# Cross-attention in 64 software-pipelined slots: u's halves made sooner, the mask on ScalarE, and the inputs of the first slots normalised ahead of A's turns

## The reference

```
# block 0: c = channels (128), t and s = positions (512)
Mn = Wn @ inorm(x) + bn;  Mm = Wm @ inorm(ctx) + bm
A  = softmax(Mn^T Mm)                        # 512 x 512, per item
x1 = Wo @ ((Wl @ ctx + bl) A^T) + bo + x
# block 1: 128 queries and 128 keys of 512 features, 16 heads of 32
q = layer_norm(x1) @ q_w + q_b;  k = ctx @ k_w + k_b;  v = ctx @ v_w + v_b
hidden = softmax(q k^T / sqrt(32), masked) v @ cproj_w + cproj_b + x1
out = hidden + gelu(layer_norm(hidden) @ fc_w + fc_b) @ proj_w + proj_b      # fc: 512 -> 2048
```

## Time and profile before

| | |
|---|---|
| median of 3 runs | 3034.93 us (3034.04 to 3037.51) |
| profiled execution | 3036.39 us, span 3034.5 us |
| granted clock of PE, mean | 0.984 of full speed |
| busy, share of the span | PE 94%, PE weight loads 78%, DVE 63%, ACT 48%, POOL 37% |
| DMA | 416.65 MB, mean 137 GB/s |

### The profile page before, as it was taken

One profiled execution on the slowest core, in us unless ns is written; L12 is line 12 of the kernel. 1 busy time (PEld: TensorE's weight loads), 2 busy tenths in 40 slices (PEclk: granted clock), 3 DMA queues, 4 the chain that ended last, 5 costly groups with the idle time before them and its releaser, 6 DMA issues. The chain is left out here.

```text
span 3034.5 us, 54536 instructions
## 1 busy us (share of the span) xinstructions
PE 2864.3 (94%) x17527; PEld 2369.3 (78%) x17527; DVE 1910.4 (63%) x3705; ACT 1469.5 (48%) x4210; POOL 1119.3 (37%) x998
## 2 busy tenths in 40 slices
PE   5899999999999999999977999999999999999999
PEld 3777777777777777777765888888888888888887
DVE  5799899999989899999855433333333333333332
ACT  5788778887878877888743211111111111111111
POOL 5566666666666666666632000000000000000000
PEclk7999999999999999999997999999999999999999
DMA  6588888888888888888863210101111111011110
GB/s 184 164 237 230 231 238 229 239 229 235 232 227 237 228 235 236 232 235 232 226 175 129 69 40 17 41 28 41 41 41 41 29 27 39 30 41 41 41 28 14
DMA packets 440889, 416.65 MB, mean 137 GB/s; under 512 B 155200, under 2 KB 319552, under 8 KB 440768
## 3 DMA queue, kind: packets, MB, share of 16 engines
q1 hardware_dynamic: 440768, 415.40, 49.4%
HBM read 231.79 MB, written 167.77 MB: 132 GB/s over the span
## 5 line engine op out<-in xcount | busy, mean ns | idle before, releaser
L1306 ACT ACTIVATE gl<-pre,fc_bias 128x512 f32<-128x512 f32 x256 | 176.6, 690 | 1119.4 <-PE pre L1391 1119.4
L1345 DVE CAST hT_hi<-gl 128x512 fp32r<-128x512 f32 x256 | 109.3, 427 | 840.2 <-ACT gl L1306 840.2
L673 ACT ACTIVATE rows<-bank,negmax 128x128 f32<-128x128 f32 x1024 | 364.2, 394 | 209.2 <-DVE negmax L829 198.9
L599 POOL TENSOR_TENSOR at_lo<-a_blocks,at_hi 128x512 fp32r<-128x512 f32 x256 | 335.4, 1330 | 190.1 <-ACT at_hi L710 190.1
L590 POOL TENSOR_TENSOR rows<-rows,rsum 128x512 f32<-128x512 f32 x256 | 266.0, 1040 | 271.4 <-DVE rsum L825 271.4
L177 POOL TENSOR_TENSOR rstd<-ve,neghalf 128x4 f32<-128x4 f32 x16 | 16.3, 1018 | 870.9 <-DVE ve L171 870.9
L1390 PE MATMUL pre<-yT_hi,rest_lo 128*128 128x512 f32 x768 | 298.9, 389 | 0.0
L1389 PE MATMUL acc<-rest_lo,hT_hi 128*128 128x512 f32 x768 | 298.9, 389 | 0.0
L1391 PE MATMUL acc<-rest_hi,hT_hi 128*128 128x512 f32 x768 | 298.9, 389 | 0.0
L1391 PE MATMUL pre<-yT_hi,rest_hi 128*128 128x512 f32 x768 | 298.8, 389 | 0.0
L1389 PE MATMUL pre<-yT_lo,rest_hi 128*128 128x512 f32 x768 | 298.8, 389 | 0.0
(11 more groups left out here) (158 smaller groups left out, 7886.1 us busy)
## 6 DMA issues: line engine op xcount, KB each, us to landing
a_turn<-rows SPq DMA_DIRECT2D x128, 512.0 KB, 7.6
a_blocks<-a_turn SPq DMA_DIRECT2D x256, 256.0 KB, 5.0
p_turn<-rows SPq DMA_DIRECT2D x128, 512.0 KB, 4.5
p_blocks<-p_turn SPq DMA_DIRECT2D x256, 256.0 KB, 5.9
x_ctx<-in_x SPq DMA_DIRECT2D x64, 256.0 KB, 2.6
x_ctx<-in_ctx SPq DMA_DIRECT2D x64, 256.0 KB, 2.9
blocks<-in_ctx SPq DMA_DIRECT2D x256, 64.0 KB, 5.5
small<-in_x SPq DMA_DIRECT2D x64, 256.0 KB, 5.9
```

The source lines that it names most:

```text
L599: pool.tensor_tensor(by_rows(at_lo, j), a_chunks[:, j], by_rows(at_hi, j).bitcast(F32), ALU.subtract).then_inc(at_lo_set, 1)
L673: act.activation(probs[:, :, r, c, :], by_chunk(S1_BANK[r])[:, c, :].rearrange("p (d b) -> p d b", b=32), ACT.Exp, bias=negmax1[:, r, c:c ...
L1306: act.activation(gl[:, i % 2, :], pre[i % 2][:], ACT.Gelu_apprx_tanh, bias=mlp.fc_bias[:, i:i + 1]).then_inc(gelu_done, 1)
```

## The change

Six edits:

1. ACT makes u_hi after the first of the four scalings of A, no longer after the fourth.
2. DVE makes u_lo ahead of the normalising of the next inputs and of the last two turns of A, no longer behind both.
3. The mask minus 1 moves from DVE to ACT, where it stands behind the upper halves of the next inputs and ahead of ctxT_hi. It takes a bias of -1 from a new constant, and the count of constants goes from 3 to 4.
4. In slots 0 to 4 (`filling`) DVE takes the statistics of the next inputs ahead of the maxima of S0, and normalises them right behind the inverted sums, ahead of A's turns.
5. In the same slots ACT makes their upper halves ahead of the scalings of A, and POOL their lower halves ahead of at_lo.
6. The halves of k's weights stand on POOL behind the lower halves of the inputs; those of v's weights, which stood at the head of slot 1 on ACT and POOL, stand on ACT behind M's halves and on POOL behind the lower halves of the inputs.

```diff
@@ POOL @@
+                filling = b0.exists() and not b4.exists()
...
-                if b0.first():
-                    lower_halves(K_W)
+                def lower_normed():
+                    if ahead.exists():
+                        for i in range(2):
+                            pool.wait_ge(normed_hi_set, ahead.nth(2, i + 1))
+                            pool.tensor_tensor(normed_lo[:, i, :], normed[:, i, :],
+                                               normed_hi[:, i, :].bitcast(F32), ALU.subtract).then_inc(normed_lo_set, 1)
...
+                if filling:
+                    lower_normed()
+                if b0.first():
+                    lower_halves(K_W)
+                if a1.first():
+                    lower_halves(V_W)
                 lower_at(0)
                 lower_at(1)
...
+                if not filling:
+                    lower_normed()
@@ ACT @@
                 if b0.first():
                     upper_halves(K_W)
+                if a1.first():
+                    upper_halves(V_W)
...
+                if filling:
+                    upper_normed()
                 if b0.exists():
                     act.wait_ge(rsum0_set, b0.nth(1, 1))
-                    for t in range(DC):
-                        act.activation(A[:, :, t, :], A[:, :, t, :], ACT.Identity,
-                                       scale=rsum0[:, t:t + 1]).then_inc(a_scaled, 1)
+                scale_a(0)
                 if b1.exists():
                     act.wait_ge(u_done, b1.nth(1, 1))
                     act.activation(u_hi, bank[U_BANK][:], ACT.Copy).then_inc(u_hi_set, 1)
+                scale_a(1)
+                scale_a(2)
+                scale_a(3)
                 upper_at(0)
...
+                if not filling:
+                    upper_normed()
+                if b3.exists():
+                    if b3.first():
+                        act.wait_ge(consts_set, 4)
+                    act.wait_ge(mask_loaded[b3.parity], b3.dma())
+                    if b3.has_before(1):
+                        act.wait_ge(s1_done, (b3 + -1).nth(1, 1))
+                    act.activation(mask_less_1[:], mask_u8[:, b3.parity, :], ACT.Identity,
+                                   bias=minus_one[:]).then_inc(mask_set, 1)
@@ DVE @@
+                if filling:
+                    input_statistics()
                 sum1_reciprocal(1)
...
-                if ahead.exists():
...
+                if not filling:
+                    input_statistics()
                 if b0.exists():
                     dve.wait_ge(exp0_done, b0.nth(4, 4))
                     if a1.exists():
                         dve.wait_ge(a_scaled, a1.nth(4, 4))
                     dve.reciprocal(rsum0[:], sum0[:]).then_inc(rsum0_set, 1)
+                if filling:
+                    normalise_inputs()
                 turn_a(0)
                 turn_a(1)
...
-                turn_a(2)
-                turn_a(3)
                 if b1.exists():
                     dve.wait_ge(u_hi_set, b1.nth(1, 1))
                     lower(u_lo, bank[U_BANK][:], u_hi, u_lo_set)
+                if not filling:
+                    normalise_inputs()
+                turn_a(2)
+                turn_a(3)
...
-                    dve.tensor_scalar(mask_less_1[:], mask_u8[:, b3.parity, :], -1.0, None,
-                                      ALU.add).then_inc(mask_set, 1)
```

More of the change, by code:

```diff
@@ L640, in first_group @@
                     mlp.lower_half(pool, mlp.first_lo[:, 1, c, :], mlp.first_hi[:, 1, c, :], 1, c, mlp_raw[1])
-            slots(pool, slot, {1: lambda: lower_halves(V_W), LAST: first_group})
+            slots(pool, slot, {LAST: first_group})
         @block.scalar
@@ L706, in slot, with upper_normed @@
                     upper_halves(C_W)
+                def upper_normed():
+                    if ahead.exists():
+                        for i in range(2):
+                            act.wait_ge(normed_set, ahead.nth(2, i + 1))
+                            act.activation(normed_hi[:, i, :], normed[:, i, :], ACT.Copy).then_inc(normed_hi_set, 1)
                 def upper_at(j):
@@ L836, in maximum0, with input_statistics, normalise_inputs @@
                                           negate=True).then_inc(max0_set, 1)
+                def input_statistics():
+                    if ahead.exists():
+                        u = ahead.parity
+                        dve.wait_ge(x_loaded[u], ahead.dma())
+                        dve.bn_stats(in_stats[:, 0, :], x_in).then_inc(in_stat, 1)
+                        dve.wait_ge(ctx_loaded[u], ahead.dma())
+                        dve.bn_stats(in_stats[:, 1, :], ctx_in).then_inc(in_stat, 1)
+                        dve.wait_ge(in_stat, ahead.nth(2, 2))
+                        dve.sem_inc(stats_seen, 1)
+                        for i in range(2):
+                            dve.bn_aggr(in_mv[:, i, :], in_stats[:, i, :]).then_inc(in_aggr, 1)
+                        dve.wait_ge(in_aggr, ahead.nth(2, 2))
+                        dve.tensor_scalar(in_ve[:], in_mv[:, :, 1], EPS, None, ALU.add).then_inc(in_veps, 1)
+                def normalise_inputs():
+                    if ahead.exists():
+                        dve.wait_ge(in_rstd_ready, ahead.nth(1, 1))
+                        if b0.exists():
+                            dve.wait_ge(m_done, b0.nth(2, 2))
+                            dve.wait_ge(normed_lo_set, b0.nth(2, 2))
+                        for i, src in enumerate((x_in, ctx_in)):
+                            dve.tensor_scalar(normed[:, i, :], src, in_mv[:, i, 0:1],
+                                              in_rstd[:, i:i + 1], ALU.subtract, ALU.mult).then_inc(normed_set, 1)
                 def turn_a(j):
@@ L905, in slot @@
                     lower(outT_lo, bank[PV_BANK][:], outT_hi, outT_lo_set)
[L906 to L913, removed]
-                                          in_rstd[:, i:i + 1], ALU.subtract, ALU.mult).then_inc(normed_set, 1)
-                turn_a(2)
-                turn_a(3)
                 if b1.exists():
```

26 lines of the change are left out of this document (10 added, 16 removed).

## The result

The changed kernel takes 3041.15 us in the median (3037.51 to 3050.27, 14 runs), the one before 3034.91 (3031.45 to 3038.14, 14 runs): ratio 1.0023, 95% interval 1.0015 to 1.0030. The medians differ by 6.2 us, slower, where 2.2 us less were forecast. The profiled execution of after took 3045.41 us (span 3043.6), 4.3 over its median, so it shows somewhat more of the trouble than most.

A forecast was written before the change was run, and what follows sets the result against it. Rings through PE and POOL, ending within about 0.1 us, were taken to bound the 23.63 us slot. Terms 0 + 4.8 + 0 + 3 - 3 - 4.5 - 2.5 = -2.2 us from 3034.93 gave 3032.7 us; 8-in-10 range 3019 to 3050.

The forecast's parts named there:

- The two rings: Full slots: dependency loops through PE and through POOL close within about 0.1 us; shortening PE's alone gains nothing.
- the lock between ctxT_lo and x1n: Shared ports: x1n on DVE stands until POOL's ctxT_lo is over, so takes 1.43 us and ends about 0.3 after it.
- The wait before out0: PE's wait for u_lo in full slots, 65.0 us in all: it goes, but PE waits before x1n's turn instead.
- u_hi's wait: ACT waits 0.17 us for u after the first scaling, in half the slots: +4.8 us.
- The mask: Mask moved from DVE to ACT behind normed_hi, with only ctxT_hi behind it: cost 0, bounds 0 and 22 us.
- The trip of A: A's way through DRAM, now also hanging on u_lo: late blocks cost +3 us.
- The 0.58 us of delay: On DVE the normalising moves back by u_lo's length, so A's blocks land 0.58 us later.
- a cushion: Turns of A: u_lo is 1.0 us ahead of need, so a late turn is absorbed up to that.
- rival C: Late A blocks put the second normalising behind POOL's at_lo in half the slots: about +20 us, 3055; chance 0.16.
- What goes: Full slots: 1.1 us of late turns and about 2 us for one 1.8 us wait disappear, -3 us.
- the drain: Last slots, where nothing is normalised and PE waits 6.3 us for u_lo: -2.5 us, bounds 0 and -6.3.
- The first slots: Earlier normalising and moved weights' halves bring the first x1 to about 63.3 us: -4.5 us in sum, bounds 0 and -10.

The follow-up runs named there:

- both_rings: old_norm_place with POOL also waiting for x1n before it begins ctxT_lo: 2996.37 us, ratio 0.9878 to the kernel before.
- norm_first: The changed kernel with only the normalising of the inputs put ahead of u_lo again on DVE; u_hi stays behind the first scaling: 3033.52 us, 0.9993.
- old_norm_place: u_hi_second with the normalising of the inputs ahead of u_lo again on DVE: 3028.47 us, ratio 0.9975 to the kernel before.
- mask_only: The kernel before with only the mask moved from DVE to ACT: 3034.89 us, ratio 1.0003.
- write_first: u_hi_second with A's write put ahead of the loads in SP's queue, the normalising still late: 3028.68 us, ratio 0.9979 to the kernel before.
- u_hi_second: The changed kernel with u_hi on ACT behind the second scaling of A instead of the first: 3045.87 us, ratio 1.0040 to the kernel before.
- pool_and_write: pool_waits with A's write put ahead of the loads in SP's queue: 2987.12 us, ratio 0.9845 to the kernel before.
- pool_waits: The changed kernel with POOL waiting for x1n before it begins ctxT_lo: 3079.19 us, ratio 1.0147 to the kernel before.
- start_undone: old_norm_place with the first five slots as in the kernel before: 3031.36 us, ratio 0.9988 to the kernel before.
- no_start: The changed kernel with the first five slots as in the kernel before: 3043.83 us, ratio 1.0037 to the kernel before.
- start_only: The kernel before with only the first slots of the changed kernel: 3033.95 us, ratio 1.0000.

## Why the prediction was wrong, step by step

- The two rings and the lock between ctxT_lo and x1n: right. The wait before out0 went, 0.84 us appeared before the turn, the gain was none. both_rings against the two single edits shows it as a pair: either ring alone holds the slot. The Trainium skill, "SBUF — State Buffer", "Who interferes with whom" (the one that issues first keeps the pair of ports for its whole instruction), is borne out from the other side as well: with POOL held back, x1n takes 0.55 us.
- u_hi's wait, +4.8: right; +5.05 (norm_first against old_norm_place).
- The mask, 0: right for the time on before, -0.2 us (mask_only), within what can be measured. But that only ctxT_hi stands behind it was wrong: PE waits for it in every slot of after, and 7.7 us up to 165 us, where before had the 3.6 us of the earlier trace rows and I had added 0.55.
- The trip of A, +3: **the step that failed**. It measured +7.6 (after against norm_first). The 0.58 us of delay was right (0.84 in SP's wait, 0.46 in the wait for A's write), but I let most slots "bear it" and gave late turns a cushion. The cushion protects u_lo. It does not protect the second normalising, which in an undisturbed slot starts about 0.9 us ahead of POOL's at_lo (2.95 against 3.86 us behind the inversion): with blocks later than that the cost goes up by a step, and a slot loses 1.2 to 2.6 us at once. I had priced a tail as if it were proportional, and put the step into rival C alone as a thing of half the slots or none. That it is the order in SP's queue through which the late normalising costs is shown where A's write goes first and the normalising stays late: -17.2 us (write_first against u_hi_second) and -92 (pool_and_write against pool_waits). After with that edit alone was not run.
- What goes, -3, and the drain, -2.5: together -5.5, measured -3.9 (start_undone against before). How they share it is not measured. The wait for u_lo in the drain, 6.3 us in the earlier trace rows, has mostly stayed in after:

```profile
PE bank L1006 <- DVE m_lo L840: 5.1, 4, 1.5
```

- The first slots, -4.5: too large; -2.9 (old_norm_place against start_undone), with -2.7 and -1.1 in the other two pairs (after and no_start, start_only and before). The first x1 comes at 65.38, not 63.3: the turns of slot 2 waited for A's blocks until 61.76, while before's began at 60.28, where I had them 0.8 to 0.9 earlier. DVE's row of after, and then four stretches of before and of after (columns: window, length, busy us of PE, PEld, DVE, ACT, POOL, granted clock, DMA share, GB/s):

```profile
61.76 1.30 DVE L902 STREAM_TRANSPOSE a_blocks<-a_blocks 128x512 f32<-128x512 f32 x2 [6.19 <-DMA a_blocks<-a_turn]
```

```profile
50.00:73.00 23.00, 17.09 (x79) 13.43 (x78) 15.33 (x29) 10.69 (x22) 12.66 (x12) 0.76 0.53 146
58.00:60.00 2.00, 2.00 (x20) 1.96 (x19) 0.11 (x2) 1.85 (x3) 0.69 (x1) 1.00 0.95 205
60.00:63.00 3.00, 1.95 (x16) 1.86 (x15) 2.72 (x4) 2.24 (x5) 1.21 (x1) 0.71 0.05 14
73.00:95.00 22.00, 18.00 (x94) 14.94 (x92) 16.71 (x31) 15.32 (x31) 10.55 (x11) 0.92 0.51 144
```

```profile
50.00:73.00 23.00, 17.86 (x77) 14.48 (x76) 11.99 (x23) 10.69 (x21) 14.08 (x13) 0.67 0.49 138
58.00:60.00 2.00, 1.60 (x10) 1.51 (x9) 0.00 (x0) 1.23 (x3) 0.35 (x1) 0.60 1.04 230
60.00:63.00 3.00, 0.00 (x0) 0.00 (x0) 1.24 (x3) 0.50 (x1) 0.00 (x0) 0.50 0.50 176
73.00:95.00 22.00, 17.97 (x91) 15.20 (x90) 16.72 (x30) 14.82 (x31) 9.64 (x10) 0.87 0.53 144
```

Since its work was pulled forward, PE ran out of it earlier: in after it stood before u_lo for 4.09 us up to 63.69, in before for 3.30 up to 65.25. The granted clock fell to 0.50, the level of 1.2 GHz, while PE was still working: between 58 and 60 us in after, after 60 us in before. It stayed there past 71 us in both, so longer in after. From 73 to 95 us it is 0.84 to 0.89 in every profile with the new start and 0.90 to 1.00 with the old; from 50 to 73 us the two groups overlap (0.65 to 0.75 and 0.72 to 0.78). How much of the 4.5 us went to this clock, to the late blocks and to the waits for the mask is not separated by any run.

The measured terms can't be added up as a check. Between after and before lie norm_first, old_norm_place and start_undone, and the differences along this chain, 7.6 + 5.05 - 2.9 - 3.6 (with the before of the first series), give 6.2 by themselves; the mask's -0.2 is inside the last one. What they do tell is the share of each step, each from runs made beside different runs of before.

## What to carry to other kernels

A delay of half a microsecond is not priced by its own length: look for what is queued behind the delayed wait, above all in a queue of transfers served in order, and for the next lock or deadline it may cross. Where two rings have one length, test edits in pairs; one alone shows nothing, and the third ring, here the trip through DRAM, decides whether the pair brings 38 us or costs as much. Put a transfer whose data is ready ahead of one that waits.

## What the runs showed that I had not expected

- The same added wait on POOL is worth -2.0 us on before (within the noise), -32.1 on old_norm_place and +38.0 on after.
- Late blocks feed themselves: in pool_waits one caught normalising delays the next slot's write, and long slots follow each other; in after they mostly stand alone.
- The spread of a kernel's times tells of it: 3034.89 to 3059.81 us over 12 runs with the trip at its limit (u_hi_second), 3027.14 to 3029.93 over 11 with A's write first (write_first).
